# A causal mask on transposed scores: 256 TensorE matmuls replaced by selections on the pool engine

## The chip, the cores and the metric

The kernel is one program on one core of a Trainium2 chip. The metric is its device time in microseconds (us), from the first to the last instruction of one execution with what lies around it. Most executions agree within 0.3%. An engine is named as in the profile: PE is TensorE, DVE VectorE, ACT ScalarE, POOL GpSimd, SP the engine that issues DMAs.

## The reference, cut to what matters

Four transformer layers run one after the other over four sequences of 512 tokens with 128 features. The change lies in the first half of the second layer (L1): self-attention with 16 heads of 8 features, and a causal mask.

```
scores = jnp.einsum('bqhd,bkhd->bhqk', Q, Kp) / jnp.sqrt(jnp.float32(HD))
if causal:
    mask = jnp.tril(jnp.ones((Sq, Sk), bool))
    scores = jnp.where(mask, scores, -jnp.inf)
a = jax.nn.softmax(scores, axis=-1)
o = jnp.einsum('bhqk,bkhd->bqhd', a, V)
```

Query q may look at key k only for k <= q. The other attentions (cross attention to 154 context tokens in L0 and L1, quantised attention in L2, grouped attention in L3), the experts and the feed-forward layers have no causal mask of this kind.

## The kernel before, in words

The work is cut into units: one sequence in one stage. Units 0 to 3 are the cross attention of L0, 4 to 7 the causal self-attention (SELF), 8 to 11 the cross attention of L1. These twelve are the "exact" units, where every factor is split in bf16 parts. Each engine runs its own program in a fixed order, and the engines meet at semaphores.

The scores are computed twice. `scores_exact` makes them with the queries on the partitions, only so that DVE can take the maximum of each row (`top_exact`, L1680). Here the mask stays a matmul of the identity with `causal` (L898), before and after. Four small DVE instructions then split the maxima of a group of four heads in three bf16 parts (`split_tops`, L1689 to L1692), TensorE transposes them (the item `tops`, L787) and ACT copies them (L1225). `scores_transposed` makes the scores again with the keys on the partitions: keys times queries (L922), the mask (L924), minus the row maxima through a matmul with `ones` (L926). ACT takes the exponential of one bank of 128x512 (L1287) into one of twelve buffers `expT`; `weigh_batch` multiplies these by the values (L949), which sums over keys in `acc`.

A causal unit has four groups of four heads, and each group ten slots: slots 0 to 3 hold the first 128 keys of one head each (one piece of 512 queries, diagonal block in the first 128 columns); slots 4 to 7 hold the second key tile (384 queries) and the fourth (128 queries) of one head; slots 8 and 9 hold the third key tile (256 queries) of two heads. A piece's diagonal block is always its first 128 columns, so there are 4 + 12 = 16 mask matmuls a group, 64 a unit, 256 in all. Batches to be weighed are slots 0 to 3, 4 to 7, and 8 with 9; they are weighed in slot 5, in slot 9, and in slot 1 of the next group.

The order in a slot w on TensorE is: transposed scores of w (they wait for the exponential of w-2, as there are two banks), then one or two steps of `scores_exact` for the group after this one (eight steps a group, in slots 0 to 6, the last two both in slot 6; a step waits for the maximum of the step two before), then the items that a table gives for this slot, then the weighing. The items are the small parts of a unit: K, Q, V projections, N1, r, N2 (softmax sums and normalising), W (output projection and residual), M (layer norm's result), H (transpose), cna, cnb, cnc (the statistics and the norm of the context). They pass through one bank `misc` in a fixed order. For a causal unit the items of the unit before it and the next one lie at K 1, Q 2, N1 3, V 4, r 5 to 8, N2 9, W 10, M 12, H and cna 14, cnb 15, cnc 17, and `tops` in slots 8, 18, 28, 38 (slots counted through the unit). POOL takes part in few: in W it raises the variance to -0.5 (L1839), in M it makes two additions or multiplications of 128x512 (L1900, L1843), in cna a small power (L1910).

Before the change POOL's program goes through the items alone, with no word of slots: it waits at each item for the semaphores of that item. The first block of the program (L583 to L656) loads the constants through SP, clears buffers on POOL and casts constants on DVE, and all engines join at its end.

Of the kernel before, what the change touches and what calls it, by code (L numbers as in the profile page):

```python
# [6 lines left out]
B, TOKENS, CTX, D = 4, 512, 154, 128  # L7
P = 128
# [8 lines left out]
LOWEST = -1.0e30  # L17
GROUPS = HEADS // 4
PAIRS = HEADS // 2
SLOTS = 12  # L20
# [34 lines left out]
L0, SELF, CROSS, MOE, QSELF, QCROSS, FF0, GQA, FF1 = range(STAGES)  # L55
# [15 lines left out]
def is_causal(u):  # L71
    return stage(u) == SELF
# [21 lines left out]
STEP_BASE, BLOCKS, BATCHES, BATCH_BASE, FIRST_SLOT = {}, [], [], {}, {}  # L94
# [10 lines left out]
EXACT_SLOTS = len(BLOCKS)  # L105
# [168 lines left out]
BEFORE, EXACT_ITEMS, MOE_ITEMS, QUANT_ITEMS, FF0_ITEMS, GQA_ITEMS, FF1_ITEMS, AFTER = SCHEDULE  # L274
# [42 lines left out]
def build(nc, io, out):  # L317
# [3 lines left out]
    with ctx:  # L321
        def sb(name, shape, dt=fp32):
            return ctx.enter_context(nc.sbuf_tensor(name, shape, dt))

        def sem(name):
            return ctx.enter_context(nc.semaphore(name))
# [2 lines left out]
        ident = sb("ident", [P, P])  # L329
        ident_half = sb("ident_half", [P, P], fp16)  # L330
        ident_bf = sb("ident_bf", [P, P], bf16)
        causalT = sb("causalT", [P, P], bf16)
        causal = sb("causal", [P, P], bf16)
        q_bias = sb("q_bias", [P, 2])
        head_mask = sb("head_mask", [P, 4])
# [180 lines left out]
        top_split = sem("top_split")  # L516
        scoresT_ready = sem("scoresT_ready")
        expT_ready = sem("expT_ready")
        weighed = sem("weighed")
        acc_copied = sem("acc_copied")  # L520
        oT_ready = sem("oT_ready")
# [59 lines left out]
        FIRST_SEQUENCE_LOADS, REST_LOADS = 4, 2  # L581

        with nc.Block() as once:  # L583
            causal_f, causalT_f = y[:, 0, 0, :], y[:, 0, 1, :]
            loads = [(ident[:, :], io["ident"]), (sizes[:, :], io["sizes"].partition_broadcast(P)), (cols[:, :], io["cols"]),
                     (causal_f, io["causal"]), (causalT_f, io["causalT"]), (head_mask[:, :], io["head_mask"]),
                     (attn_w[:, 0:4, :], io["attn_w"][:, 0:4, :])]
            late_loads = [(rows[:, :, :], io["rows"].partition_broadcast(P)), (norm_sel, io["norm_sel"]),
                          (attn_w[:, 4:20, :], io["attn_w"][:, 4:20, :]), (expert_no[:, :], io["expert_no"]),
# [41 lines left out]
            @once.vector  # L631
            def _(dve):
                dve.wait_ge(cleared, 4)
                for j in range(4):
                    nc.vector.memset(ones[32 * j:32 * j + 3, j, :], 1.0)
                    nc.vector.memset(ones_tail[32 * j:32 * j + 3, 32 * j:32 * j + CTX_TAIL], 1.0)
                for n in range(3):
                    nc.vector.memset(ones_pad[32 * n:32 * n + 1, :], 1.0)
                for j in range(4):
                    rows_j = slice(32 * j, 32 * j + CTX_TAIL)  # L640
                    for i in range(2):
                        at_col = i * (P + HD) + 32 * j + 16
                        nc.vector.memset(v_tail[rows_j, :, at_col:at_col + HD], 1.0)
                nc.vector.memset(minus_half[:, :], -0.5)
                dve.wait_ge(weights_in, 16 * len(loads))
                nc.vector.tensor_copy(ident_half[:, :], ident[:, :])
                nc.vector.tensor_copy(ident_bf[:, :], ident[:, :])
                nc.vector.tensor_copy(causal[:, :], causal_f)
                nc.vector.tensor_copy(causalT[:, :], causalT_f)
                nc.vector.reciprocal(inv_sizes[:, :], sizes[:, :])  # L650
                for n, name in enumerate(["L1_xattn_sa_bq", "L1_xattn_ca_bq"]):
                    nc.vector.tensor_scalar(q_bias[:, n:n + 1], col(name), float(HD) ** -0.5, None, ALU.mult)
                for n in range(2):
                    q, k, vv, w = (sizes[:, 4 * n + i:4 * n + i + 1] for i in range(4))
                    nc.vector.tensor_scalar(exp_scale[:, n:n + 1], q, k, float(HD) ** -0.5, ALU.mult, ALU.mult)
                    nc.vector.tensor_scalar(out_scale[:, n:n + 1], vv, w, None, ALU.mult)  # L656
        with nc.Block() as block:
# [69 lines left out]
            def _(pe):  # L727
# [174 lines left out]
                def scores_transposed(w):  # L902
                    u, g, _, pieces = BLOCKS[w]
                    if w >= 2:
                        pe.wait_ge(expT_ready, w - 1)
                    if w == 0 or BLOCKS[w - 1][1] != g:
                        pe.wait_ge(misc_read, out_of("tops", u, g))
                    bank = trans[w % 2]
                    for j, k, q0, c0 in pieces:
                        n = TOKENS - q0  # L910
                        if j is None:
                            pe.wait_ge(k_tail_ready, seq(u) + 1 + (B if stage(u) == CROSS else 0))
                            for z in range(2):
                                nc.tensor.matmul(bank[:, :], k_tail[:, u % 2, g, z * P:(z + 1) * P],
                                                 q_stack[:, u % 2, 2 * g + z, :], start=(z == 0), stop=False)
                            ins = nc.tensor.matmul(bank[:, :], ones_tail, top_rows[:, g % 2, :],
                                                   start=False, stop=True)
                            continue
                        h = 4 * g + j
                        keys = (k_half_ctx if is_cross(u) else k_half)[:, u % 2, h % 2, h // 2, k * P:(k + 1) * P]  # L920
                        dst = bank[:, c0:c0 + n]
                        nc.tensor.matmul(dst, keys, q_stack[:, u % 2, h // 2, q0:TOKENS], start=True, stop=False)  # L922
                        if is_causal(u):
                            nc.tensor.matmul(bank[:, c0:c0 + P], ident_bf[:, :], causalT[:, :],  # L924
                                             start=False, stop=False)
                        ins = nc.tensor.matmul(dst, ones[:, j, :], top_rows[:, g % 2, q0:TOKENS],  # L926
                                               start=False, stop=True)
                    ins.then_inc(scoresT_ready, 1)

                def weigh_batch(n):  # L930

                    u, g, w0, blocks = BATCHES[n]
                    b, half = n - BATCH_BASE[u], (2 if is_cross(u) else 6)
                    pe.wait_ge(expT_ready, w0 + len(blocks))
                    if b == 0:
                        pe.wait_ge(misc_read, out_of("V", u))
                        if u:
                            pe.wait_ge(acc_copied, 2 * u)
# [890 lines left out]
            def _(pool):  # L1829
# [94 lines left out]
                        nc.gpsimd.tensor_tensor(gq_qT[:, b % 2, n, :], gq_qT[:, b % 2, n, :], turn[:, n % 2, :], ALU.add)\  # L1924
                            .then_inc(gq_q_ready, 1)

                for table in (BEFORE, EXACT_ITEMS, MOE_ITEMS):
                    for slot in sorted(table):
                        for it in table[slot]:
                            item(*it)  # L1930

                def of_step(z, i):
                    u, t, a, h, heads = quant_step(i)
# [50 lines left out]
def constants():  # L1984
    c = {}
    c["ident"] = np.eye(P, dtype=np.float32)
    q, k = np.arange(P)[:, None], np.arange(P)[None, :]
    c["causal"] = np.where(k > q, LOWEST, 0.0).astype(np.float32)
    c["causalT"] = np.where(q > k, LOWEST, 0.0).astype(np.float32)
    c["head_mask"] = (np.arange(P)[:, None] // HD % 4 == np.arange(4)[None, :]).astype(np.float32)  # L1990
    sel = np.zeros((P, 4, P), np.float32)
    for n in range(2):
# [54 lines left out]
```

## Time and profile before

| | us |
|---|---|
| median of 3 runs | 1835.81 (1832.58 to 1836.81) |
| profiled execution | 1836.09 |
| its span | 1834.3 |
| of it: up to the first causal slot | 228 |
| causal units | 254 (228 to 482) |
| cross units of L1 | 178 (482 to 660) |

Over the span PE is busy 1499.2 us (82%), DVE 1119.3 (61%), ACT 947.8 (52%), POOL 585.3 (32%). Busy time of matmuls is their way through the pipeline, and successive ones overlap in it; so the start of one to the start of the next is the better measure of what one costs. The mean granted TensorE clock is 0.864.

### The profile page before, as it was taken

Reading aid. Unit: us, or ns where it says so; the run is one execution under the profiler, and the core shown is the slowest. Engines: PE = TensorE matmul, PEld = TensorE weight load, DVE = VectorE, ACT = ScalarE, POOL = GpSimd, SP = SyncE. Lnnn points to the kernel's source line nnn. Section 1 sums busy time; section 2 is a strip of 40 time slices with the busy share of each in tenths; the row PEclk is TensorE's granted clock in tenths of the full one; section 3 lists DMA queues with packets and bytes.
Section 4 is the critical chain, followed back from the end, with each engine's and each line's share of the span. In section 5 each row is a group of like instructions: output and inputs, shape, how many; then the busy total and the mean of one; then the engine's idle time right before and its main releaser. Section 6 shows DMA issues by size and latency. Waiting matters only on the chain.

```text
span 1834.3 us, 31467 instructions
## 1 busy us (share of the span) xinstructions
PE 1499.2 (82%) x10850; PEld 884.3 (48%) x10912; DVE 1119.3 (61%) x3147; ACT 947.8 (52%) x2486; POOL 585.3 (32%) x979
## 2 busy tenths in 40 slices
PE   2678888888877799999877787777778878888888
PEld 2344444454433357777544444444445443544545
DVE  2456666666555533333489999987775555565533
ACT  1334444544534344544478778787775243444541
POOL 4111000001011100110177677776664144344420
PEclk9899999999989899999956665655556989999989
DMA  5222231132062100000200000000000000000000
GB/s 163 42 42 58 48 64 41 30 59 43 22 125 43 29 1 1 1 1 1 90 3 2 1 2 2 1 2 1 1 2 1 1 1 8 1 8 1 1 1 23
DMA packets 30877, 44.29 MB, mean 24 GB/s; under 512 B 8696, under 2 KB 23680, under 8 KB 28544
## 3 DMA queue, kind: packets, MB, share of 16 engines
q1 hardware_dynamic: 27808, 40.06, 10.1%
q10 hardware_dynamic: 2912, 2.22, 0.4%
q8 instruction: 88, 1.44, 0.3%
q14 instruction: 69, 0.57, 0.1%
HBM read 33.94 MB, written 8.32 MB: 23 GB/s over the span
## 4 chain that ended last, share of the span: by engine, by line
PE 53%; DVE 21%; ACT 15%; issue 8%; POOL 2%; ACTq 0%; DMA 0%; SPq 0%; POOLq 0%; DVEq 0%
ACT arena L1330 10%; PE trans L988 6%; PE score L977 6%; DVE minus_top L1680 4%; PE acc L949 3%; PE misc L863 3%; PE misc L797 3%; DVE top_score L1743 3%; PE trans L926 2%; PE trans L922 2%; PE score L888 2%; PE misc L803 2%; DVE arena L1803 2%; PE acc L947 2%; PE score L1116 2%
## 5 line engine op out<-in xcount | busy, mean ns | idle before, releaser
L1330 ACT ACTIVATE arena<-score,minus_top,exp_scale 128x512 f32<-128x512 f32 (+1 forms) x512 | 315.9, 624 | 23.2 <-POOL arena L1952 5.8
L1680 DVE TENSOR_REDUCE minus_top<-score 128x4 f32<-128x616 f32 (+4 forms) x256 | 198.0, 806 | 195.9 <-PE score L892 70.0
L1952 POOL TENSOR_SCALAR arena<-arena,inv_total 128x512 f16<-128x512 f32 (+1 forms) x512 | 280.8, 548 | 79.5 <-DVE inv_total L1750 41.8
L1839 POOL TENSOR_TENSOR rstd<-spread,minus_half 128x4 f32<-128x4 f32 x36 | 36.7, 1018 | 750.2 <-DVE spread L1411 675.7
L1287 ACT ACTIVATE arena<-trans 128x512 f32<-128x512 f32 x240 | 141.3, 597 | 161.8 <-PE trans L926 158.2
L1743 DVE TENSOR_REDUCE top_score<-score 128x2 f32<-128x1024 f32 (+1 forms) x192 | 206.3, 1074 | 1.7 <-PE score L1018 1.0
L1034 PE MATMUL trans<-ident_half,arena 128*128 128x128 f16 x1536 | 185.1, 295 | 7.1 <-POOL arena L1952 7.1
L1018 PE MATMUL score<-arena 32*128 32x512 bf16 (+1 forms) x512 | 98.3, 432 | 107.5 <-ACT arena L1330 105.8
L1368 ACT ACTIVATE arena<-arena,minus_top 128x154 f32<-128x154 f32 x256 | 105.1, 412 | 155.8 <-DVE minus_top L1808 155.6
L1034 PEld LDWEIGHTS trans<-ident_half,arena 128*128 128x128 f16 x1536 | 137.5, 133 | 72.0 <-POOL arena L1952 35.8
L1298 ACT ACTIVATE arena<-score,b_cols 128x512 f32<-128x512 f32 x128 | 86.9, 687 | 108.9 <-PE score L977 108.6
L988 PEld LDWEIGHTS trans<-late,arena 128*128 128x128 f32 x1024 | 124.1, 192 | 29.7 <-issue 29.4
L1732 DVE TENSOR_SCALAR arena<-trans 128x1024 bf16<-128x1024 f16 x192 | 131.1, 683 | 2.3 <-PE trans L1034 1.8
L988 PE MATMUL trans<-late,arena 128*128 128x128 f32 x1024 | 124.3, 275 | 0.0
L926 PE MATMUL trans<-arena 128*128 128x512 bf16 (+3 forms) x377 | 120.6, 329 | 2.0 <-issue 0.9
L1716 DVE SCALAR_TENSOR_TENSOR y<-trans,combine,y 128x128 f32<-128x128 f32 x128 | 36.0, 344 | 139.4 <-PE trans L988 139.4
L977 PE MATMUL score<-hT,late 128*128 128x512 f32 x256 | 120.7, 595 | 0.0
L888 PE MATMUL score<-arena 128*128 128x154 bf16 x512 | 71.6, 250 | 54.9 <-issue 50.1
L1972 POOL TENSOR_TENSOR arena<-arena,inv_total 128x512 f32<-128x512 f32 x64 | 66.5, 1040 | 130.6 <-DVE inv_total L1816 120.1
L1321 ACT ACTIVATE minus_top<-top_score,exp_scale 128x2 f32<-128x2 f32 (+1 forms) x192 | 56.9, 296 | 85.3 <-DVE top_score L1743 82.9
L1330 ACT ACTIVATION_READ_ACCUMULATOR arena<-score,minus_top,exp_scale 128x1 f32 x512 | 100.4, 196 | 0.0
L1018 PEld LDWEIGHTS score<-arena 32*128 32x128 bf16 x512 | 21.3, 101 | 163.9 <-ACT arena L1330 142.2
(252 smaller groups left out, 2936.1 us busy)
## 6 DMA issues: line engine op xcount, KB each, us to landing
arena<-q_terms SPq DMA_DIRECT2D x176, 64.0 KB
q_terms<-arena SPq DMA_DIRECT2D x36, 128.0 KB
late<-k_terms SPq DMA_DIRECT2D x64, 64.0 KB
arena<-k_terms_ctx SPq DMA_DIRECT2D x112, 20.0 KB
late<-in_L_xattn_e_w SPq DMA_DIRECT2D x1, 2048.0 KB, 18.3
k_terms<-arena SPq DMA_DIRECT2D x12, 128.0 KB
arena<-in_mask_Bx1xSxS_ff SPq DMA_DIRECT2D x4, 308.0 KB, 5.5
rows<-in_rows SPq DMA_DIRECT2D x1, 1024.0 KB, 8.7
```

The source lines that it names most:

```text
L888: ins = nc.tensor.matmul(dst, q_stack[:, u % 2, c, t * P:(t + 1) * P], k_half_ctx[:, u % 2, s, c, 0:CTX], start=True, stop=(stage(u) != L0))
L926: ins = nc.tensor.matmul(dst, ones[:, j, :], top_rows[:, g % 2, q0:TOKENS], start=False, stop=True)
L977: nc.tensor.matmul(up_bank[n % 4], e_w1[:, e, c * P:(c + 1) * P], hT[:, b, :], start=True, stop=True)\
L988: ins = nc.tensor.matmul(trans[n % 2][:, t * D:(t + 1) * D], e_h[:, n % 2, c, t * P:(t + 1) * P], e_w2[:, e, c, :], start=(c == 0), stop=( ...
L1018: ins = nc.tensor.matmul(score[i % 2][:, j, z * n:(z + 1) * n], qT_codes[r:r + 32, u % 2, t * P:(t + 1) * P], k4_codes[r:r + 32, u % 2, h ...
L1034: ins = nc.tensor.transpose(trans[i % 2][:, :].bitcast(fp16)[:, of], codes[:, i % 2, j, first:first + P], ident_half[:, :])
L1287: nc.scalar.activation(expT[w % SLOTS], trans[w % 2][:, :], ACT.Exp, bias=bias)\
L1330: ins = nc.scalar.activation(probs[:, i % 2, j, of], score[i % 2][:, j, of], ACT.Exp, bias=minus_top[:, at_col:at_col + 1], scale=exp_scal ...
L1680: nc.vector.tensor_reduce(dst, src, axis=AX.X, op=ALU.max, negate=True).then_inc(top_ready, 1)
L1732: nc.vector.tensor_scalar(pT_codes[:, i % CODE_SLOTS, :, :].rearrange("p k q -> p (k q)"), trans[i % 2][:, :].bitcast(fp16)[:, 0:2 * P * T ...
L1743: nc.vector.tensor_reduce(of_step(top_score, i), src, axis=AX.X, op=ALU.max, negate=True).then_inc(quant_top, 1)
L1952: ins = nc.gpsimd.tensor_scalar(codes[:, (i - 1) % 2, j, of], probs[:, (i - 1) % 2, j, of], inv_total[:, at_col:at_col + 1], HALF_ROUND, A ...
```

## The change

The mask matmul L924 goes, and with it the constant `causalT`, its load and its cast. In its place POOL goes over each causal slot in order: it waits until the exponential of slot w is there and sets the part of the diagonal block or blocks above the diagonal (keys after the query) to zero, in place, with one `affine_select`: over 128 columns where the slot has one piece, over two blocks of 128 columns where it has two. A new semaphore `expT_selected` counts them, and `weigh_batch` of a causal unit waits for the count of its last slot. POOL's program through the exact units is now by slots: the selection of slot w, then the items of slot w.

```
--- before.py
+++ after.py
-        causalT = sb("causalT", [P, P], bf16)
...
+        expT_selected = sem("expT_selected")
...
-            causal_f, causalT_f = y[:, 0, 0, :], y[:, 0, 1, :]
+            causal_f = y[:, 0, 0, :]
...
-                     (causal_f, io["causal"]), (causalT_f, io["causalT"]), (head_mask[:, :], io["head_mask"]),
+                     (causal_f, io["causal"]), (head_mask[:, :], io["head_mask"]),
...
-                nc.vector.tensor_copy(causalT[:, :], causalT_f)
...
-                        if is_causal(u):
-                            nc.tensor.matmul(bank[:, c0:c0 + P], ident_bf[:, :], causalT[:, :],
-                                             start=False, stop=False)
...
+                    if is_causal(u):
+                        pe.wait_ge(expT_selected, w0 + len(blocks) - FIRST_SLOT[SELF * B])
...
-                for table in (BEFORE, EXACT_ITEMS, MOE_ITEMS):
-                    for slot in sorted(table):
-                        for it in table[slot]:
-                            item(*it)
+                zero = nc.gpsimd.to_reg(0.0)
+
+                def select(w):
+
+                    starts = [c0 for _, _, _, c0 in BLOCKS[w][3]]
+                    z = expT[w % SLOTS]
+                    if len(starts) == 1:
+                        z, pattern = z[:, 0:P], [[1, P]]
+                    else:
+                        z = z.rearrange("p (a q) -> p a q", q=P)[:, ::starts[1] // P, :]
+                        pattern = [[0, 2], [1, P]]
+                    pool.wait_ge(expT_ready, w + 1)
+                    nc.gpsimd.affine_select(out=z, in_=z, pattern=pattern, compare_op=ALU.is_ge, fill=zero, base=0,
+                                            channel_multiplier=-1).then_inc(expT_selected, 1)
+
+                for it in BEFORE[0]:
+                    item(*it)
+                for w in range(EXACT_SLOTS):
+                    if is_causal(BLOCKS[w][0]):
+                        select(w)
+                    for it in EXACT_ITEMS.get(w, ()):
+                        item(*it)
+                for slot in sorted(MOE_ITEMS):
+                    for it in MOE_ITEMS[slot]:
+                        item(*it)
```

## Rows read from the trace of the kernel before

**Rows 1.** Windows by stage: stretch, its us, busy us of each engine, PEclk, DMA share, GB/s.
```profile
228.00:482.00 254.00, 221.47 (x1947) 126.48 (x1976) 163.98 (x356) 122.85 (x214) 18.20 (x20) 0.99 0.22 43
```
**Rows 2.** Groups by line, causal stage, PE: count, busy us, mean ns, idle before.
```profile
L924 PE MATMUL trans<-causalT,ident_bf 128*128 128x128 bf16 x256 | 56.1, 219 | 0.6 <-issue 0.2
```
**Rows 3.** Timeline, PE, slot 4 of a group: start us, length us, instruction.
```profile
303.17 0.22 PE L922 MATMUL trans<-arena,late 128*128 128x128 bf16 x1
...
303.45 0.22 PE L896 MATMUL score<-late,arena 128*128 128x128 bf16 x1
```
**Rows 4.** Chain of waits, causal stage, by line; and waits there (us, times, longest).
```profile
by line: DVE minus_top L1680 14.4%; PE acc L949 14.0%; PE trans L922 9.4%; PE trans L926 7.7%; PE score L896 7.6%; PE misc L797 6.9%; issue 6.4%; PE trans L924 3.5%; PE score L898 3.3%; PE misc L787 2.4%; PE misc L781 1.7%; DVE normed L1427
...
PE misc L787 <- DVE arena L1692: 24.7, 16, 1.6
```
**Rows 5.** Chain of waits in order of time, 228 to 300 us: start, us, what.
```profile
252.66 0.96 PE misc L812 x8
...
265.94 0.38 PE misc L787 x4
...
279.28 0.38 PE misc L787 x4
...
292.62 0.38 PE misc L787 x4
```
**Rows 6.** Timeline of a quiet group.
```profile
284.48 2.59 DVE L1680 TENSOR_REDUCE minus_top<-score 128x2 f32<-128x768 f32 x3 [0.91 <-PE score L898]
...
284.97 0.60 ACT L1287 ACTIVATE arena<-trans 128x512 f32<-128x512 f32 x1 [0.33 <-PE trans L926]
...
286.79 0.10 PEld L896 LDWEIGHTS score<-late,arena 128*128 128x128 bf16 x1 [0.17 <-DVE minus_top L1680]
...
287.23 1.06 PE L949 MATMUL acc<-arena 128*32 128x512 f32 x8
...
289.42 2.09 DVE L1680 TENSOR_REDUCE minus_top<-score 128x2 f32<-128x768 f32 x2 [1.40 <-PE score L898]
...
290.51 1.15 ACT L1287 ACTIVATE arena<-trans 128x512 f32<-128x512 f32 x2 [0.93 <-PE trans L926]
...
291.55 0.20 DVE L1689 CAST arena<-minus_top 128x16 bf16<-128x16 f32 x1
```
**Rows 7.** Timeline, slots 12 to 16 of the first causal unit.
```profile
259.78 1.28 POOL L1843 TENSOR_TENSOR x<-x,rows 128x512 f32<-128x512 f32 x1
259.97 1.06 PE L949 MATMUL acc<-arena 128*32 128x512 f32 x8
262.76 2.08 DVE L1680 TENSOR_REDUCE minus_top<-score 128x2 f32<-128x768 f32 x2
```
**Rows 8.** Timelines, POOL and DVE, unit 1; then groups by line, causal stage, DVE.
```profile
47.29 1.27 POOL L1843 TENSOR_TENSOR x<-x,rows 128x512 f32<-128x512 f32 x1 [10.05 <-PE misc L739]
47.75 0.87 DVE L1689 CAST arena<-minus_top 128x16 bf16<-128x16 f32 x1
...
L1541 DVE TENSOR_TENSOR ctx_spread<-ctx_moments 128x2 f32<-128x2 f32 x4 | 2.2, 552 | 0.1
```
**Rows 9.** Groups by line and shape, whole span, POOL.
```profile
L1952 POOL TENSOR_SCALAR arena<-arena,inv_total 128x512 f16<-128x512 f32 x256 | 177.6, 694 | 21.4
L1952 POOL TENSOR_SCALAR arena<-arena,inv_total 128x154 f16<-128x154 f32 x256 | 103.2, 403 | 58.2 <-DVE inv_total L1750 41.8 <-POOL x L1843 1.6
L1854 POOL TENSOR_TENSOR rows<-rows 128x128 f32<-128x128 f32 x2 | 0.9, 452 | 3.1 <-DMA router_b<-in_router_b 3.0
L629 POOL MEMSET arena<- 128x256 f32 x2 | 0.6, 311 | 0.0
```
**Rows 10.** Timeline, DVE, end of the first block; SP's loads there.
```profile
9.97 0.23 DVE L646 CAST ident_half<-ident 128x128 f16<-128x128 f32 x1 [5.54 <-DMA attn_w<-in_attn_w]
...
10.39 0.22 DVE L649 CAST causalT<-y 128x128 bf16<-128x128 f32 x1
...
2.59 0.43 SPq L598 DMA_DIRECT2D y<-in_causalT  x1
```

More of the change, by code:

```diff
@@ L1988, in constants @@
     c["causal"] = np.where(k > q, LOWEST, 0.0).astype(np.float32)
-    c["causalT"] = np.where(q > k, LOWEST, 0.0).astype(np.float32)
     c["head_mask"] = (np.arange(P)[:, None] // HD % 4 == np.arange(4)[None, :]).astype(np.float32)
```

## The prediction

> **What bounds the kernel now.** I read the windows by stage first, to see which engine fills the causal stage; then the chain of waits in it, the timeline of a few microseconds, and the POOL and DVE rows of the whole trace. The stage runs from 228 to 482 us: 16 head groups in 160 slots, TensorE busy 221 of 254 us at nearly full clock, DVE 164, ACT 123, POOL 18 [rows 1]. TensorE is not alone on the path: the chain gives 14.4% of the stage to the row maxima on DVE (L1680), and TensorE waits 16 times, once a group and 24.7 us together, for L1692, the last step of splitting these maxima [rows 4, 5]. A group in its quiet form runs from one L787 to the next, 279.28 to 292.62 us: 13.34 us [rows 5].
>
> **What is removed.** 256 mask matmuls [rows 2]. Each is listed with 219 ns, but that is its way through the pipeline. In the timeline five such steps lie between 303.17 and 303.45, an L924 the second of them: 0.056 us each [rows 3], with the weight loads beside. All 256 at 0.056 are 14.3 us, the upper bound. The chain charges L924 with 3.5% of 254 us, 8.9 us [rows 4]. Even that is too much, since the chain names one of two that end together. So I count by slot, 16 masks a group.
>
> In a quiet group DVE begins the maxima of score step 2 at 284.48 and is busy without a gap for 2.59 us; TensorE's step 5 at 286.79 waits for it, 0.17 us already now [rows 6]. Masks of slots 3, 4 and 5 (five) lie under that. Steps 6 and 7 start DVE at 289.42; from there 2.09 us of maxima and four small splits lead to L787 at 292.62 [rows 5, 6]. Masks of slots 7 and 8 (four) lie under that. On the path are slots 0 to 2, 6 and 9: three, two and two, so seven. This holds for groups 2 and 3 of each of the four sequences. In group 0 slot 3 lies beside ACT's copy of Q, which N1 waits for; slot 5 beside DVE's copy of V, slot 9 beside the copy before N2; slot 4, ahead of V, counts instead: seven again. In group 1 everything from the output projection at 252.66 to L787 at 265.94 is a DVE chain (residual, statistics, normalisation, context statistics, maxima) [rows 5]; only the mask of its slot 0 and the two of slot 9 count: three. That is 24 a sequence, 96 in all, 96 x 0.056 = 5.4 us. At the start one cast goes (9.97 to 10.39 for three, 0.14 us each) and one 64 KB load, 0.43 us of SP's issue ahead of that of attn_w, which DVE waits for [rows 10]; between 0.1 and 0.6, I take 0.4. Gain: 5.8 us.
>
> **What is added on POOL.** 160 selections in place: 64 over 128 columns, 96 over 256. No row shows this operation. By the nearest form, one tensor input, f32, L1952 takes 403 ns for 154 columns and 694 for 512 [rows 9], so by the line through them 0.38 us for 128 and 0.49 for 256. From below: a MEMSET that reads nothing takes 311 ns for 256. From above: a two-input TENSOR_TENSOR takes 1.28 us for 512 [rows 7] and 452 ns for 128, so 0.73 for 256; a software test for each element could cost more still, and I keep twice that, 1.45, as an unlikely far end. The sum, 64 x 0.38 + 96 x 0.49 = 71 us, fits beside the 18 of 254. Below nothing is excluded for the engine itself, since no POOL work is taken away.
>
> **The new wait.** The last batch before a weighing needs its selection. In quiet groups the tightest place is slot 5: the exponential of slot 3 ends at 284.97 + 0.60 = 285.57 and L949 starts at 287.23 [rows 6], so 0.6 us of hand-over and selection is hidden. It is not in slot 5 of group 1. There POOL does M: two operations of 1.28 us, the second until 261.06, and in program order the selection of slot 3 (the 13th) stands behind them. TensorE weighs at 259.97 now [rows 7]. A hand-over between engines I estimate at 0.08, twice the step within DVE from 291.51 (289.42 + 2.09) to 291.55 [rows 6]. Afterwards: 261.06 + 0.08 + 0.38 + 0.08 = 261.6. Queued behind the waiting L949 are the weighing, the transposed scores of slot 6 and score step 6, on which DVE's L1680 waits: in the quiet group 2.19 us from L949 (287.23) to L1680 (289.42) [rows 6]. So, less two masks, DVE begins at 263.7 what it begins at 262.76 [rows 7]: 0.9 us, four times, 3.6 us. The power of `cna` also moves behind two selections, but by less, and beside it.
>
> **POOL against DVE.** This is what I weigh most. At 47.29 POOL starts an add of 1.27 us; DVE's cast L1689, 0.20 us in the quiet group [rows 6], starts at 47.75 and takes 0.87, until POOL is done. L1541, two columns and both inputs in SBUF, takes 552 ns in all its four runs, since it comes while M's L1843 is running on POOL [rows 7, 8]. So small SBUF operations of DVE stand still while POOL works.
>
> *The Trainium skill says so too ("SBUF — State Buffer", section "Who interferes with whom"): a DVE instruction with two SBUF inputs, or a cast in a two-port mode, and a GpSimd instruction exclude each other for the whole instruction, while tensor_reduce never contends. By that rule the exchange is not free here; had the ports been independent, the sum would be 5.8 gained less the 3.6 of the M wait: -2.2, 1833.9 us, which stands under rival (b).*
>
> In each group the last two exponentials, back to back, end at 291.66, and the splits start at 291.55 [rows 6]. Without two masks in slot 7 they end 0.1 earlier. Selection 7 then runs to about the start of the splits, and selection 8 begins at 291.63 at the earliest, or as the first cast ends; L1690, with two SBUF inputs, meets it and waits 0.3 to 0.5 us: I take 0.40. TensorE waits for these splits in every group, so nothing hides it. Step 7 sets both off, so the spacing returns in nearly every group (the wait for the splits is 24.7 us in 16 times, the longest 1.6 [rows 4]); 15 x 0.40 = 6.0 us. In group 1 the four L1427 of the normalisation (1.1 us together, on the DVE chain) meet the selections of slots 1 and 2, released when POOL ends rstd: 0.5 us each time, 2.0 us. The splits of Q and K in group 0 meet selections as well, with 0.4 us of slack on DVE: nothing.
>
> **The sum.** -5.4 - 0.4 + 3.6 + 6.0 + 2.0 = +5.8 us. The profiled execution took 1836.1 (span 1834.3 and 1.8 around it), 0.3 above the median of the runs. So 1841.9 by the profile, 1841.6 against the median. Stages after 482 us should only move.
>
> *By the Trainium skill ("GPSIMD Engine Reference", section "3.1 Elementwise — side-by-side cycle accounting") a tight loop takes about 1.8 cycles an element at 1.2 GHz; an estimate from it is 0.38 us for 256 columns without dispatch, which with some dispatch is near what I take. The sum would be the same. No row here shows it for this operation.*
>
> **Rivals.**
> (a) Faster, the collisions do not matter: POOL's selections are as short as the MEMSET (0.31 us), so that selection 7 is over before the splits and selection 8 fits nearly beside the first cast. For it: one input tensor and no arithmetic. Against: POOL's operations that read SBUF are all dearer than its MEMSET [rows 9], and the one in [rows 8] held DVE to its end. Then -8.9 (the chain's share) - 0.4 + 3.3 = -6.0, 1830.1 us; with all masks paid and no M wait (-14.3 - 0.4), 1821.4.
> (b) No change: gains as counted or somewhat more, half of the collisions, since who comes first in each is a matter of 0.1 us: -5.8 - 1.8 + 3.6 + 4.0 = 0, 1836 us. No collision at all gives -2.2 and belongs here. Against it: L1689 and L1541.
> (c) Much slower, the selection at the two-input price or above. At 0.73 us the selection of slot 7 holds back the first cast and that of slot 8 the next: about 2 x 0.73 - 0.5 = 0.96 us a group, 14 us, plus 3 for the normalisation and 4 for M, less 5.8: +15, 1851 us. It decides from 0.5 us on, where each further 0.1 us costs 0.2 a group. At 1.45 it would be nearly 40 more, and slots of 1.0 us would be paced by POOL: 1880.
> (d) The change does something else: before, the mask made zeros inside ACT's exponential; now the exponential may overflow where it is selected away. The two exponentials at 290.51, with masked columns, take 1.15 us, and the one at 284.97 takes 0.60 [rows 6]: ACT's time follows the columns, not the values, so nothing in it.
>
> **Chances.** Differences under 0.2% (3.7 us) cannot be told from none. The forecast with its own range 1839.5 to 1846 has 0.40; (c) 0.18, slower too; (b) 0.22, same; (a) 0.20, faster. Slower 0.58, same 0.22, faster 0.20. The range reaches half way into (a) and past (c)'s first value: 1828 to 1856.
>
> **What would show it.** No L924; the transposed scores' steps 0.056 us closer. 160 selections on POOL in the stage, 0.38 and 0.49 us: above 0.6 speaks for (c), below 0.35 for (a). L1690 or L1689 stretched from 0.2 us to 0.5 us and more in nearly every group, and the quiet group still about 13.34 us (-0.39 + 0.40): 13.0 says (a), 13.9 says (c). L949 waiting for POOL in slot 5 of group 1 and nowhere else. The stage 254 us long, give or take, grows by 6. It would be wrong if DVE's splits kept their lengths, or if stages after 482 us changed their length.

## The result, and the profile after

The changed kernel takes 1838.49 us (median of 20 runs, 1833.1 to 1846.52), the kernel before 1832.49 in as many beside them (1819.92 to 1836.81): ratio 1.0036 [1.0023, 1.005], so 4 to 9 us slower, where 1.0032 was forecast. The median itself lies inside the outer range of the forecast (1828 to 1856) and 1 us below its inner one (1839.5 to 1846), because the kernel before came out 3 us lower in 20 runs than in the three that the forecast started from. One run of the kernel before, made beside the last two experiments (2004.87 us at a clock of 0.712), was in a slower state and is left out of every comparison. The profiled execution took 1835.08 us (span 1833.4, granted clock 0.862). That is one us less than the profiled one of before, though the medians differ by 6.6 the other way; a single pair of profiles cannot carry the total here, and stage lengths are read together with the clock in them.

The causal stage and its four sequences (columns: stretch, its us, busy us and instructions of PE, PEld, DVE, ACT, POOL, granted clock, DMA share, GB/s), then two stretches of half clock in it, and a stretch with one quiet group in it:
```profile
226.60:490.70 264.10, 217.46 (x1698) 113.93 (x1723) 166.32 (x356) 120.30 (x213) 76.01 (x180) 0.95 0.21 41
226.60:292.60 66.00, 54.21 (x433) 28.46 (x437) 42.66 (x90) 30.32 (x53) 18.69 (x44) 0.98 0.24 45
292.60:361.30 68.70, 56.76 (x430) 29.21 (x436) 42.55 (x90) 30.25 (x54) 18.82 (x44) 0.92 0.22 43
361.30:428.90 67.60, 55.64 (x432) 29.08 (x437) 42.57 (x90) 30.19 (x54) 18.84 (x44) 0.94 0.21 44
428.90:490.70 61.80, 50.85 (x413) 27.19 (x418) 38.54 (x86) 29.55 (x54) 19.67 (x48) 0.97 0.17 32
311.00:314.40 3.40, 3.40 (x8) 0.88 (x10) 1.07 (x3) 0.15 (x1) 0.41 (x1) 0.50 0.51 77
324.60:328.00 3.40, 3.03 (x14) 0.89 (x15) 1.45 (x5) 0.09 (x1) 1.64 (x4) 0.51 0.52 84
331.80:344.80 13.00, 10.70 (x99) 5.84 (x101) 7.30 (x12) 6.86 (x12) 3.65 (x10) 1.00 0.01 2
```
Before, this stage took 254 us at a clock of 0.99 [rows 1]; now it takes 264.1 at 0.95. The quiet stretch is at full clock. Seven stretches of 3.4 us run at half of it (1.2 GHz instead of 2.4); before there was one. Such a stretch is called a spell below. So two things are to be kept apart: how long a group takes at full clock, and how many spells fall in the stage.

The chain of waits in order of time (start, us, what) gives the groups; `tops` is at L786 now:
```profile
245.32 1.98 PE misc L796 x4
...
263.39 0.38 PE misc L786 x4
276.35 0.38 PE misc L786 x4
289.31 0.38 PE misc L786 x4
309.64 0.40 PE misc L786 x4
310.70 3.53 PE misc L796 x4
331.84 0.38 PE misc L786 x4
344.81 0.38 PE misc L786 x4
```
Quiet groups take 276.35 - 263.39 = 12.96 us and 344.81 - 331.84 = 12.97, where they took 13.34 [rows 5]. The same four products of N1 (L796) take 1.98 us in the first sequence and 3.53 at 310.70, inside a spell. Group 0 from 289.31 to 309.64 takes 20.33 us with a spell and 18.70 in a run below without one; group 1 from 309.64 to 331.84 has two spells and takes 22.20, against 19.12 without. A spell costs some 1.5 to 1.7 us of its 3.4.

The waits of the stage (us, times, the longest), the chain in it by line, and the groups of POOL's selections by shape (busy us, mean ns, idle before and what ended it):
```profile
PE misc L786 <- DVE arena L1690: 28.0, 16, 1.9
PE acc L947 <- POOL arena L1937: 6.1, 4, 1.5
```
```profile
by line: DVE minus_top L1678 18.0%; PE acc L947 16.4%; PE trans L922 7.5%; PE trans L921 7.3%; PE misc L796 7.2%; issue 6.8%; PE score L895 6.2%; PE score L897 2.9%; PE misc L786 2.3%; POOL x L1841 1.9%; POOL x L1898 1.9%; PE misc L780 1.8%
```
```profile
L1937 POOL TENSOR_SCALAR_AFFINE_SELECT arena<-arena 128x256 f32<-128x256 f32 x96 | 39.5, 411 | 102.0 <-ACT arena L1285 101.0
L1937 POOL TENSOR_SCALAR_AFFINE_SELECT arena<-arena 128x128 f32<-128x128 f32 x64 | 19.0, 300 | 80.5 <-ACT arena L1285 80.2
```
The mask's share [rows 4] is gone, the maxima have 18.0% instead of 14.4, and POOL's two operations of M are on the chain for the first time, 1.9% each. The weighing waits for POOL four times, as forecast, up to 1.5 us. A selection costs 0.30 us over 128 columns and 0.41 over 256, less than the 0.38 and 0.49 taken. The wait for the splits is 28.0 us instead of 24.7.

The end of a quiet group (timeline: start, us, instruction, count, idle before), to be laid beside [rows 6]:
```profile
273.96 1.22 DVE L1678 TENSOR_REDUCE minus_top<-score 128x2 f32<-128x1024 f32 x1
274.56 0.59 ACT L1285 ACTIVATE arena<-trans 128x512 f32<-128x512 f32 x1
275.21 0.20 DVE L1687 CAST arena<-minus_top 128x16 bf16<-128x16 f32 x1
275.22 0.45 POOL L1937 TENSOR_SCALAR_AFFINE_SELECT arena<-arena 128x256 f32<-128x256 f32 x1
275.45 0.26 DVE L1688 TENSOR_TENSOR arena<-minus_top,arena 128x16 f32<-128x16 f32 x1
275.74 0.20 DVE L1689 CAST arena<-arena 128x16 bf16<-128x16 f32 x1
```
The last exponential ends at 275.15 and the selection starts at 275.22, 0.01 after the first cast and beside it, not behind it. It ends at 275.67; L1688 ends at 275.71 and takes 0.26 where it took 0.18. That is all that is left of the collision: 0.08 us a group, where 0.40 was forecast.

*The Trainium skill ("SBUF — State Buffer", section "Who interferes with whom") has a DVE instruction with two SBUF inputs contend with a GpSimd one that reads SBUF, and the trace agrees: L1688 is held to the selection's end. It also has a cast in a two-port mode and a GpSimd instruction block each other fully, the one that is issued first going first. Where a selection is first, in group 1 (262.52, in the next fence), the cast L1689 is held to its end, 0.35 us, as the rule says. Here the cast, first by 0.01 us, kept its 0.20, as the rule says too; but the selection took 0.45 instead of 0.41, so only 0.04 us of a hold on it can be seen, and no run here shows whether it was blocked for the rest of the cast or had not yet come to its reading.*

Slots 12 to 16 of the first causal unit and the splits behind them, to be laid beside [rows 7] (same columns; the last row is the same weighing one sequence later, in a spell):
```profile
253.64 1.11 DVE L1425 TENSOR_SCALAR normed<-y,moments,rstd 128x128 f32<-128x128 f32 x4
...
256.19 1.26 POOL L1841 TENSOR_TENSOR x<-x,rows 128x512 f32<-128x512 f32 x1
...
256.92 0.55 DVE L1539 TENSOR_TENSOR ctx_spread<-ctx_moments 128x2 f32<-128x2 f32 x1
...
257.52 0.67 POOL L1937 TENSOR_SCALAR_AFFINE_SELECT arena<-arena 128x128 f32<-128x128 f32 x2
...
257.97 1.07 PE L947 MATMUL acc<-arena 128*32 128x512 f32 x8 [1.52 <-POOL arena L1937]
...
260.05 2.09 DVE L1678 TENSOR_REDUCE minus_top<-score 128x2 f32<-128x768 f32 x2 [0.53 <-PE score L897]
...
262.52 0.41 POOL L1937 TENSOR_SCALAR_AFFINE_SELECT arena<-arena 128x256 f32<-128x256 f32 x1 [0.42 <-ACT arena L1285]
...
262.63 0.35 DVE L1689 CAST arena<-arena 128x16 bf16<-128x16 f32 x1
...
324.97 1.94 PE L947 MATMUL acc<-arena 128*32 128x512 f32 x8 [1.52 <-POOL arena L1937]
```
This is the forecast wait: M's second operation ends at 257.45, two selections follow it back to back, L947 starts 0.52 after M's end (0.54 forecast), and DVE's maxima of steps 6 and 7 wait 0.53 for what stands behind it. The four instructions of the normalisation (L1425) take 1.11 us, which is what the forecast took for before, although two selections run from 253.34 to 253.89, beside the first of them.

### The profile page after: what moved, and what is told of

Same layout as the page of the kernel before. It is cut to its first block, busy times and chain, and to the rows that moved or that the text cites. A ratio compares the mean times of both kernels' runs of the same rounds, so it can differ in the third digit from the quotient of the medians.

```text
span 1833.4 us, 31163 instructions
## 1 busy us (share of the span) xinstructions
PE 1487.1 (81%) x10599; PEld 867.8 (47%) x10656; DVE 1121.0 (61%) x3146; ACT 945.3 (52%) x2486; POOL 643.1 (35%) x1139
## 4 chain that ended last, share of the span: by engine, by line
PE 53%; DVE 21%; ACT 14%; issue 7%; POOL 2%; DMA 1%; SPq 1%; ACTq 0%; POOLq 0%; DVEq 0%
ACT arena L1328 10%; PE trans L986 6%; PE score L975 6%; DVE minus_top L1678 4%; PE acc L947 4%; PE misc L862 3%; DVE top_score L1741 3%; PE misc L796 3%; PE trans L922 2%; PE misc L802 2%; PE trans L921 2%; PE score L887 2%; PE score L1114 2%; DVE arena L1801 2%; PE acc L945 2%
## 5 line engine op out<-in xcount | busy, mean ns | idle before, releaser
L1937 POOL TENSOR_SCALAR_AFFINE_SELECT arena<-arena 128x256 f32<-128x256 f32 (+1 forms) x160 | 58.4, 367 | 182.5 <-ACT arena L1285 181.1
L922 PE MATMUL trans<-arena 128*128 128x512 bf16 (+2 forms) x383 | 118.8, 334 | 4.0 <-issue 2.6
```

## The experiments

Theories: (T1) the forecast, that POOL's selections hold DVE's splits and weighing; (T2) at full clock the exchange is even, and what is lost is TensorE's clock, which falls more often in the changed kernel. The recorded expectations use letters: A, the waits lower the clock; B, fewer matmuls alone lower it (A and B are the two forms of T2); C, the same as T1. Times below are medians; "groups" are the spacings of `tops` at full clock in the order quiet / group 1 / group 0, and their sum over one sequence counts quiet twice. Before it is 13.34 / 18.14 / 18.84, together 63.66; after it is 12.96 / 19.12 / 18.70, together 63.74. Spells are counted in one profile of each kernel, and one profile need not be typical of its kernel: the table in the account sets its clock beside the mean of the timed runs.

**M later.** The changed kernel, with POOL's M moved behind the selections that queued behind it:
```
-                        item(*it)
+                        if not (causal_slot and it[0] == "M"):
+                            item(*it)
+                    if causal_slot and n == 19:
+                        item("M", BLOCKS[w][0] - 1)
```


> As the changed kernel, but POOL does the two operations of M in the causal units after the selection of slot 9 of group 1 (slot 19) instead of in slot 12, so that no selection stands behind them when TensorE wants to weigh. Theory A, the wait: in the trace after the change TensorE waits 4 times 1.52 us for a selection behind M, and the granted clock has 7 spells of 3.4 us at half speed in the stage, against 1 before; quiet groups are 12.96 us against 13.34. If these waits are what lowers the clock, both go: the groups 1 fall from 19.1 to about 17.9 us, spells to 1 or 2, and the kernel lies 3 to 7 us below before. Theory B, the density: TensorE has 256 matmuls less to do, so the clock falls whether it waits or not: spells stay at 5 to 8, only the wait itself is gained, 4 x 1.0 us, and the kernel lies 1 to 3 us above before. Theory C, POOL holds DVE (what the prediction weighed most): the same as the changed kernel less 3.6 us, so 2 to 3 us above before, with L1688 and L1689 long.

Measured: 1825.17 us against 1828.17, ratio 0.9989 [0.9963, 1.0014]. The wait of the weighing for POOL is gone, group 1 takes 18.00 us in place of 19.12, 4.5 us in four sequences. The chain in order of time, group 1 between the rows; then the end of group 1 in the first sequence:
```profile
308.18 0.40 PE misc L786 x4
...
326.18 0.38 PE misc L786 x4
```
```profile
260.60 0.41 POOL L1937 TENSOR_SCALAR_AFFINE_SELECT arena<-arena 128x256 f32<-128x256 f32 x1 [0.42 <-ACT arena L1285]
260.62 0.45 DVE L1687 CAST arena<-minus_top 128x16 bf16<-128x16 f32 x1
```
So the M wait was real. Its own price is not the whole 4.5 us, though: the move also frees the context statistics from M (L1539 takes 0.16 us where it took 0.54), and it moves the splits against the selections in group 1. Here the selection starts 0.02 us before the first cast, and the cast is held to its end, 0.45 us instead of 0.20, in all four groups 1 (splits of 1.17 us); in the quiet groups, where the cast is first by 0.01 us, it keeps its 0.20. The next experiment gives the wait alone. Two spells are left in this profile, as A expected; but it is the fastest of twelve runs and has their highest clock, 0.869, while their mean is 0.8638, as low as that of the changed kernel. The time, 2 us below before, lies between A (3 to 7 below) and B (1 to 3 above), and its interval of -6.8 to 2.6 us holds both.

**No selections, no masks** (the mask of the transposed scores is left out altogether):
```
-                    if is_causal(u):
-                        pe.wait_ge(expT_selected, w0 + len(blocks) - FIRST_SLOT[SELF * B])
...
-                    if is_causal(BLOCKS[w][0]):
-                        select(w)
```


> As the changed kernel, but with no selections and no wait for them: the transposed scores are not masked at all, so this part of the computation is left out. It shows what the 256 removed matmuls are worth alone. The prediction's own term: -5.8 us (96 of 256 on the path, and the start). Theory A (the wait lowers the clock): no more spells at half clock than before, quiet groups 12.9 us or less (12.96 less 0.08 to 0.15 in the splits), the stage 5 to 7 us shorter than before, and the kernel 5 to 8 us below. Theory B (fewer matmuls alone lower the clock): 5 to 8 spells in the stage, the gain eaten, the kernel within 3 us of before.

Measured: 1821.87, ratio 0.998 [0.9956, 1.0004]. Windows of its stage and two `tops` rows of its chain:
```profile
226.00:476.00 250.00, 212.19 (x1721) 111.43 (x1720) 163.85 (x356) 120.00 (x213) 18.22 (x20) 0.99 0.23 43
```
```profile
275.72 0.38 PE misc L786 x4
288.61 0.38 PE misc L786 x4
```
Quiet group 12.89, so 0.45 less than before (0.39 forecast), group 1 18.08 (0.06 less; 0.17 forecast), group 0 18.46 (0.38 less; 0.39). A sequence has 1.34 us less, four 5.4: the very size of the forecast's term for the masks, and far from the chain's 8.9 or the 14.3 of all steps. The changed kernel has 19.12 us in group 1, 1.04 more than here; 0.15 of that is its longer splits, so the wait behind M costs 0.89 us, 3.6 in four sequences, the forecast's own figure. Two spells fall in this profile, few as A had it; but the mean clock is lower than before's in the timed runs (0.8648 against 0.8673), and the time, 3.7 us below before (8.0 below to 0.7 above), decides between A and B no better.

**Masks and selections together**, which adds POOL's part to the kernel before. The edit puts back `causalT`, its load and its cast, and:
```
+                        if is_causal(u):
+                            nc.tensor.matmul(bank[:, c0:c0 + P], ident_bf[:, :], causalT[:, :],
+                                             start=False, stop=False)
```


> The changed kernel with the mask matmuls back as well, so both maskings are done. It shows what the selections, with their waits, cost alone. Theory A: the wait of 1.5 us in slot 5 of group 1 is there, so spells at half clock are there too, 4 or more; quiet groups 13.34 plus 0.1; the kernel 8 to 14 us above before. Theory B: TensorE has as much to do as before, the spells stay at 1 or 2, and the kernel is 4 to 6 us above before (4 x 1.0 for the waits, 16 x 0.1 for the splits). Theory C with the prediction's sizes: +11.6 us, with splits of 1.3 us instead of 0.92; the trace of the changed kernel has them at 1.0 to 1.07, so I expect this to fall.

Measured: 1834.35, ratio 1.0045 [1.0017, 1.0073], so 3 to 13 us slower.
```profile
231.00:491.00 260.00, 221.90 (x1979) 126.44 (x1978) 167.70 (x356) 122.56 (x214) 75.76 (x180) 1.00 0.22 42
```
```profile
PE acc L952 <- POOL arena L1942: 6.1, 4, 1.5
```
Groups 13.54 / 19.28 / 19.19, together 65.55: the selections cost 1.9 us a sequence, 7.6 in all, and no spell falls in the stage. The same wait for POOL, with all of TensorE's matmuls in place, went with no spell, so A's 4 or more did not come. B had the spells right and the price too low: the splits take 1.12 us in its quiet groups, a collision of 0.20 us a group where the changed kernel has 0.07, since the selection starts at another moment of them. With the masks on, taking them away is worth 65.55 - 63.74 = 1.81 a sequence, 7.2 us.

**M later, splits first.** As M later, and the selection of slot 8 waits until DVE's splits are done, so that the two never meet:
```
+                    if (w - FIRST_SLOT[u]) % PER[u] == 8:
+                        v, h = next_group(u, g)
+                        pool.wait_ge(top_split, GROUPS * v + h + 1)
```


> As m_later, and in each group the selection of slot 8 also waits until DVE has split the row maxima, so that the two no longer meet. In the trace of the changed kernel this meeting costs 0.07 to 0.15 us a group. Expected beside m_later: 16 times that, 1 to 2.4 us less, quiet groups 12.88 instead of 12.96, splits 0.92 us long throughout. If POOL held DVE for more than its rows show (theory C), 5 us or more less. If the splits are not what TensorE waits for, nothing.

Measured: 1821.69, ratio 0.9962 [0.9938, 0.9987]: 2 to 11 us faster than before. The selection in its new place (timeline), and the windows:
```profile
286.67 0.41 POOL L1941 TENSOR_SCALAR_AFFINE_SELECT arena<-arena 128x256 f32<-128x256 f32 x1 [1.13 <-DVE arena L1690]
```
```profile
225.60:474.00 248.40, 210.50 (x1729) 111.10 (x1727) 162.96 (x357) 120.53 (x214) 75.54 (x180) 0.99 0.23 44
```
Splits take 0.92 us, as before, and the quiet group 12.89: only 0.07 less than in the changed kernel. That is the whole price, in a quiet group, of the collision that the forecast put at 0.40. Against M later, group 1 gains 0.25 (17.74) and group 0 0.08 (18.62), so the sequence 0.48 and the stage 1.9 us, within the 1 to 2.4 expected.

**The changed kernel again, and with filler matmuls.** The first is the same program. The second issues six matmuls more in each causal group, of zero weights into `acc` (they add nothing), in slot 8, where TensorE waits for the splits:
```
+                    if is_causal(u) and (w - FIRST_SLOT[u]) % PER[u] == 8:
+                        for _ in range(6):
+                            nc.tensor.matmul(acc[:, :], zeros[:, :], q_stack[:, u % 2, 0, :], start=False, stop=False)
```


> The changed kernel once more, beside before on the chip of its companions, to see whether its 7 spells at half clock are its habit. In the profiles so far the stage had 1 spell before, 7 after the change, 2 with M later, 2 with neither masks nor selections, 1 with M later and the splits first, 0 with masks and selections both. Theory A (the 1.5 us waits lower the clock when TensorE has also less to do): 4 spells or more, mean granted clock of all runs 0.003 or more below that of before on the same chip, time 5 to 9 us above before. Theory B (fewer matmuls alone): 2 or 3 spells, clock 0.002 to 0.003 below as in m_later and no_select, time 2 to 4 us above. If the 7 spells were chance: no difference in the clock, time within 2 us of before, since the groups without a spell sum to +0.1 us a sequence.

> The changed kernel with 6 matmuls of zero weights, 128x128 by 512 columns, added to acc in slot 8 of every causal group, ahead of the transposition of the row maxima, where TensorE stands idle for 1.6 us anyway; 6 x 0.22 = 1.3 us fit. They change no value. At full clock the groups keep their lengths (12.96, 19.1, 18.7 us). Theories A and B both say that pauses of TensorE lower the clock: then spells in the stage fall to 0 to 2, and the kernel comes 4 to 10 us below after_again. If the granted clock does not follow TensorE's pauses in this stage: spells and time as after_again, or 1 us worse.

Measured side by side: again 1835.33, ratio 1.0031 [1.0007, 1.0054]; with filler 1830.56, ratio 1.0004 [0.9981, 1.0027]. Stage windows of the one and the other, and the filler kernel's chain:
```profile
225.00:492.00 267.00, 220.49 (x1696) 114.39 (x1721) 166.28 (x356) 120.42 (x214) 76.21 (x180) 0.94 0.21 41
```
```profile
228.00:483.00 255.00, 228.96 (x1794) 120.93 (x1824) 166.27 (x356) 120.46 (x215) 76.03 (x180) 0.99 0.22 43
```
```profile
309.63 0.40 PE misc L788 x4
...
328.75 0.38 PE misc L788 x4
341.72 0.38 PE misc L788 x4
```
Nine spells in the stage without filler, one with it, and 5.7 us above before without it, as A had both. The groups are the same at full clock (12.97 and 19.12 here), so the filler shortens nothing; it only keeps TensorE at work while it would wait, and the stage falls from 267 us to 255. This is the run that carries T2. Over the timed runs the kernel with filler is 4.8 us faster, and resampling its twelve and the other's gives 2 to 11 (4 to 10 expected); its mean clock is 0.8664 against 0.8634. The filler stands in the wait for the splits alone. The wait behind M is left, 1.5 us, and went with one spell.

**Splits first with filler**, the two edits together.

> m_later_split, the best so far (6.9 us below before, one spell in its profile), with the same 6 filler matmuls in slot 8 of each causal group. Pauses lower the clock: no spell in the stage, 1 to 4 us below m_later_split, so 8 to 11 us below before. Otherwise the same as m_later_split. Groups at full clock: 12.89, 17.7, 18.6 us.

Measured: 1820.58, ratio 0.9955 [0.9933, 0.9978]; no spell falls in the stage, which is the shortest of those shown:
```profile
229.80:476.40 246.60, 226.64 (x1790) 120.01 (x1819) 162.97 (x356) 120.31 (x213) 75.89 (x180) 1.00 0.23 44
```
Against 0.9962 without filler the filler brings nothing that can be told: that version had one spell in the stage already. The 8.2 us below before lie at the low end of the 8 to 11 expected.

**The kernel before with M later.** No selections, masks kept, M moved to the same slot.
```
+                    if causal_slot and n == 19:
+                        pool.wait_ge(expT_ready, w + 1)
+                        item("M", BLOCKS[w][0] - 1)
```


> The kernel before, masks as matmuls and no selections, with only M's two POOL operations moved from slot 12 to slot 19 in the causal units (POOL waits for that slot's exponential). It asks how much of the 7 to 9 us by which m_later_split lies below before comes from the move alone, since M's second operation holds DVE's L1541 for 0.4 us in group 1. If the move helps by this alone: groups 1 of 17.7 to 17.8 us instead of 18.14, the other groups as before (13.34 and 18.84), so 1 to 1.6 us below before, and the exchange of masks for selections is worth the other 5 to 7 us. If the move is most of it: 5 us or more below before.

Measured: 1829.49, ratio 0.9998 [0.9976, 1.002]. Group 1 takes 17.67 us instead of 18.14, since the context statistics no longer meet M:
```profile
262.29 0.16 DVE L1541 TENSOR_TENSOR ctx_spread<-ctx_moments 128x2 f32<-128x2 f32 x1
```
This row had 0.55 [rows 8]: 0.39 of the 0.47 us. But three spells fall in its stage, its mean clock is 0.8648 against 0.8671, and the whole is no faster, where 1 to 1.6 us less were expected. This kernel has all its matmuls and no selection, so neither is needed for the clock to fall. And the gain of the best version is not M's move alone.

**The best version once more**, the same program as splits first with filler.

> m_later_split_fill once more, on the same chip as before_m_later, to set the best version with selections beside the best one with mask matmuls: 8 to 10 us below before, 6 to 8 below before_m_later. If both are equal, the exchange has no worth of its own.

Measured: 1821.74, ratio 0.9961 [0.9939, 0.9984]. It stands: 3 to 11 us faster than the kernel before, where the change as made is slower. Beside the kernel before with M later, on the same chip, it is 7.8 us faster (4 to 11 by resampling, 6 to 8 expected). So the exchange has a worth once M and the splits are out of its way: 4.1 us of it at full clock (63.19 a sequence against 62.16), most of the rest by the clock (0.8673 against 0.8648). Filler was not tried in the kernel before, so what it would give there is open.

**The account.** Within one kernel, over its timed runs, a run with 0.001 less mean granted clock was 1.1 us longer (slope pooled over all kernels timed and their runs of before, each run counted once; 0.9 to 1.3 by its spread, 0.6 to 1.9 in single kernels). With it, each kernel's difference falls in two:

| | groups at full clock, 4 sequences | spells in the profile (its clock) | mean clock of the timed runs (before 0.867) | x 1.1 | sum | measured (interval) |
|---|---|---|---|---|---|---|
| change, again | +0.3 | 9 (0.859) | 0.8634 | +4.2 | +4.5 | +5.7 (1.3 to 9.9) |
| change + filler | +0.3 | 1 (0.865) | 0.8664 | +1.0 | +1.3 | +0.7 (-3.5 to 4.9) |
| no selections | -5.4 | 2 (0.867) | 0.8648 | +2.8 | -2.6 | -3.7 (-8.0 to 0.7) |
| masks and selections | +7.6 | 0 (0.873) | 0.8683 | -1.1 | +6.5 | +8.2 (3.1 to 13.3) |
| M later | -4.2 | 2 (0.869) | 0.8638 | +3.9 | -0.3 | -2.0 (-6.8 to 2.6) |
| M later, splits first | -6.1 | 1 (0.864) | 0.8668 | +0.6 | -5.5 | -6.9 (-11.3 to -2.4) |
| the same + filler | -6.0 | 0 (0.868) | 0.8679 | -0.7 | -6.7 | -8.2 (-12.3 to -4.0) |
| the same, once more | -6.0 | 0 (0.871) | 0.8673 | -0.2 | -6.2 | -7.1 (-11.2 to -2.9) |
| before, M later | -1.9 | 3 (0.864) | 0.8648 | +2.5 | +0.6 | -0.4 (-4.4 to 3.7) |

Every sum lies in its interval. The intervals are wide, however: the groups alone, without the clock, miss only that of the first row. What needs the clock is the changed kernel itself, here and in the runs beside the prediction. Those had a clock of 0.8616; against the 0.8673 of before in the later runs, which were not made beside them, that would be +6.3, with +0.3 from the groups +6.6, where 6.6 was measured. The mean clock is one of the whole execution; that its loss lies in the causal stage is seen in the profiles alone.

## Why the time came out near the forecast, and its sum did not

The time was right: +5.8 forecast, +6.6 measured, ratio 1.0032 and 1.0036. Its composition was not, and the nearness is luck: some 6 us of collisions that did not come about were made up by some 6 us of clock that the sum did not have.

- **Masks on the path, -5.4.** Right: -5.4 with neither masks nor selections (quiet groups gave a little more than counted, group 1 less), -7.2 where selections are there. The count by slots was worth its work; the 8.9 of [rows 4] and the 14.3 of all steps were far off.
- **Start, -0.4.** It came, and not smaller: TensorE's first instruction starts at 10.70 us, before at 11.58, and in all profiles at 11.6 to 11.9 in the three kernels with `causalT` and at 10.5 to 11.0 in the eight without. By the first exponential nothing of it is left in this pair (42.2 us in both); over all profiles 0.6 us is (mean 42.4 with `causalT`, 41.8 without). The sums of the account leave it out.
- **The new wait behind M, +3.6.** Right in place and in size: four waits of 1.5 us, nowhere else, and 0.89 us each for the group, 3.6 together, against the kernel without selections. (The 4.5 us by moving M hold more than the wait.)
- **"POOL against DVE", +6.0.** This step failed. It had the selection of slot 8 start at the end of the first cast and hold a later split. It starts beside the cast and holds L1688 for 0.08 us. Measured 0.07 a quiet group and 0.15 in group 1 (splits of 0.99 and 1.07 us where they took 0.92): some 1.5 us in all. Which of the two starts first decides it, by 0.01 us: where the selection was first, the cast waited for all of it (0.45 us). With the first cast free the quiet group came out at 12.96 us, not the 13.34 that stood there; by the forecast's own words, 13.0 speaks for rival (a).
- **The normalisation, +2.0.** Failed too: 1.11 us before and after.
- **The sum without clock.** From no selections to the changed kernel group 1 grows by 1.04 us, a quiet group by 0.07, group 0 by 0.24 (the forecast had nothing there): 1.42 a sequence, 5.7 in all, against 11.6 forecast. -5.4 + 5.7 = +0.3: rival (b), 1836 us.
- **What the forecast did not have** is the clock, a term that it put at nothing. It took TensorE at full clock through the stage, as [rows 1] shows it (0.99), and priced time on each side of it. The stage grew by 9.9 us, where its groups at full clock are even; six spells more at 1.5 to 1.7 us are 9 to 10. Rival (c) was wrong on the price of a selection: 0.41 us, below its threshold of 0.5. In (d) the exponential kept its length, 0.60 before and 0.59 after. One of the forecast's own signs of being wrong did come: the stages behind 482 us changed their length.

What makes a spell here is shown in part. TensorE paused for the splits at 263, 276, 289 and 309 (up to 1.9 us) and for POOL up to 1.5; a spell began at 324.6, within such a pause (the weighing starts at 324.97 after 1.52 us without work), and one at 311.0, behind the wait for the splits that ended at 309.64. Filler in the waits takes the spells away (9 to 1). The kernel with masks and selections pauses too and had no spell; the one with neither had two. Only with the masks gone and the selections and M in their places were there seven and nine, as far as single profiles can tell. Filler in the wait for the splits brought them to one with the wait behind M left, and moving M brought them to two with the wait for the splits left, so neither pause alone is shown to be the cause, and not each pause is followed by a spell. Fewer matmuls are not shown to be it either: the kernel before with M later keeps them all and had three. What sets the clock here stays open; that work in a wait raises it is shown.

Outside the stage the profile of the changed kernel is 11 us shorter than that of before. Before the stage it is 1.8 us; in the cross units 4.6, with 20.5 us at half clock instead of 34.1; behind them 4.4 at the same half-clock time. That last part is not explained here; kernels with the same code there had from 1173.6 (the changed kernel) to 1180.1 us (splits first with filler) at the same 436.9 us of half clock, so single profiles differ by that much.

## What to carry to other kernels

Where one engine's small instructions meet another engine's, a collision costs the overlap that is left after both have started, not the length of the longer; find the two start times before pricing it. A change that is even at full clock can still cost clock in a stage where TensorE pauses: look at how many stretches at half clock the stage has, and count what one costs a group. When a queue gets new work in program order, ask which long item stands ahead of it there, and move that item rather than drop the change: with that and one selection held back behind the splits, 4 to 9 us slower became 2 to 11 faster.

## What the runs showed of the hardware that was not expected

- `affine_select` in place, f32, 128 partitions: 0.30 us for 128 columns, 0.41 for two blocks of 128, below the line through the 0.40 and 0.69 of a scaling of 154 and 512 columns [rows 9]; of a buffer of 512 columns only the blocks are touched.
- Matmuls that compute nothing made a kernel faster, by the granted clock alone: with 96 more of them the stage took 255 us instead of 267 in the profiles, and the kernel 4.8 us less in the timed runs.
- A hundredth of a microsecond decides who waits: a cast on DVE that started 0.01 us before a selection on POOL kept its 0.20 us, in all eleven groups of the changed kernel where they met so; one that started 0.01 to 0.02 us after it took 0.45, in four of four.
